# First attention of a two-layer block: value products in fp32 from one exponential, in place of fp32r products of high and low parts

## The reference, cut to what matters

```python
# hidden_states (2, 1024, 512); H = 512, NH = 16 heads, HD = 32
q, k, v = proj(Wq), proj(Wk), proj(Wv)                # (B, NH, S, HD)
q = q * cos + rotate_half(q) * sin
k = k * cos + rotate_half(k) * sin
scores = einsum('bhqd,bhkd->bhqk', q, k) / sqrt(HD)
scores = where(causal, -inf, scores)                  # causal = above the diagonal
attn = softmax(scores, axis=-1)
out = einsum('bhqk,bhkd->bhqd', attn, v)              # the value products
return einsum('bsh,oh->bso', out.reshape(B, S, H), Wo)
```

## Time and profile before

| | us |
|---|---|
| median of 3 runs | 3494.87 |
| lowest, highest | 3492.46, 3495.08 |
| the profiled execution's own time | 3502.3 |
| its span (first to last instruction) | 3500.5 |
| the front, to its last large store | about 0 to 197 |
| loading of the first operands, first row maxima | 197 to 259 |
| the attention's steps, from the first Z product of head 0 to the last value product | 259 to 744 |

### The profile page before, as it was taken

One profiled execution on the slowest core, in us unless ns is written; L12 is line 12 of the kernel. 1 busy time (PEld: TensorE's weight loads), 2 busy tenths in 40 slices (PEclk: granted clock), 3 DMA queues, 4 the chain that ended last, 5 costly groups with the idle time before them and its releaser, 6 DMA issues. The chain is left out here.

```text
span 3500.5 us, 42242 instructions
## 1 busy us (share of the span) xinstructions
PE 2895.0 (83%) x14636; PEld 2302.5 (66%) x14636; DVE 2011.0 (57%) x3642; ACT 1202.6 (34%) x2343; POOL 950.9 (27%) x664
## 2 busy tenths in 40 slices
PE   7938888876999999347899999579999994488994
PEld 6825555554888888236688888467888883366773
DVE  5628778756233232435466666655666666667655
ACT  2206555542111111113344444224444442233331
POOL 1206666653111111203100000140000001267743
PEclk9958889987999999678899999899999997699997
DMA  4542222213000100672000000300000002111002
GB/s 163 196 150 70 81 96 82 76 50 114 19 19 19 36 0 1 189 278 100 26 32 31 21 31 21 131 35 25 32 21 31 21 27 102 67 37 37 0 1 96
DMA packets 111743, 224.36 MB, mean 64 GB/s; under 512 B 9376, under 2 KB 55456, under 8 KB 110848
## 3 DMA queue, kind: packets, MB, share of 16 engines
q1 hardware_dynamic: 111616, 222.72, 18.4%
HBM read 155.84 MB, written 66.58 MB: 64 GB/s over the span
## 5 line engine op out<-in xcount | busy, mean ns | idle before, releaser
L1041 POOL TENSOR_TENSOR l0a_probs_hl<-l0a_probs,l0a_probs_hl 128x896 fp32r<-128x896 f32 (+1 forms) x128 | 293.4, 2311 | 229.6 <-ACT l0a_probs L963 229.6
L1273 PE MATMUL l1a_obank<-l1a_pT_hl,l1k_v_hl 128*128 128x512 f32 (+3 forms) x1152 | 300.4, 370 | 7.2 <-DVE l1a_pT_hl L1346 7.1
L1346 DVE TENSOR_TENSOR l1a_pT_hl<-l1a_work,l1a_pT_hl 128x512 fp32r<-128x512 f32 (+3 forms) x384 | 212.9, 555 | 155.1 <-ACT l1a_pT_hl L1306 154.9
L1299 ACT ACTIVATE l1a_probs<-l1a_scores,l1a_row 128x128 f32<-128x128 f32 (+7 forms) x256 | 189.3, 741 | 317.9 <-DVE l1a_row L1336 317.9
L1253 PE MATMUL l1a_scores<-l1k_kT_hl,l1a_qa_hl 128*128 128x512 f32 (+3 forms) x1152 | 291.6, 361 | 1.5 <-ACT l1a_probs L1299 1.5
L1389 POOL TENSOR_TENSOR l1a_q_stage<-l1k_qpe,l1a_ones 128x512 fp32r<-128x512 f32 x32 | 33.3, 1040 | 875.4 <-PE l1a_work L1281 818.4
L962 ACT ACTIVATE l0a_probs_hl<-l0a_sbank 128x896 fp32r<-128x896 f32 (+1 forms) x192 | 156.2, 813 | 258.9 <-PE l0a_sbank L934 194.8
L1678 DVE TENSOR_TENSOR f0f_hid<-f0f_silu,f0f_ubank 128x512 f32<-128x512 f32 x64 | 44.1, 688 | 322.2 <-PE f0f_ubank L1613 322.2
L1306 ACT CAST l1a_pT_hl<-l1a_work 128x512 fp32r<-128x512 f32 (+3 forms) x384 | 183.6, 478 | 107.3 <-PE l1a_work L1264 106.1
L948 PE MATMUL l0a_obank<-l0a_probs_hl,l0a_v_stage 128*96 128x512 f32 (+3 forms) x768 | 195.6, 380 | 28.3 <-DVE l0a_probs_hl L1002 23.7
L1281 PE MATMUL l1a_work<-l1a_wov,l1a_oT_hl 128*128 128x512 f32 x768 | 214.2, 401 | 5.0 <-DVE l1a_oT_hl L1365 3.0
(11 more groups left out here) (254 smaller groups left out, 6324.6 us busy)
## 6 DMA issues: line engine op xcount, KB each, us to landing
qk_dram<-l0f_stage SPq DMA_DIRECT2D x8, 2048.0 KB, 9.5
l1a_wov<-wov_dram SPq DMA_DIRECT2D x32, 512.0 KB, 3.4
v_dram<-l0f_v_rows SPq DMA_DIRECT2D x16, 768.0 KB, 3.7
l0a_v_stage<-v_dram SPq DMA_DIRECT2D x8, 1536.0 KB, 9.2
l1a_wabs<-wabs_dram SPq DMA_DIRECT2D x32, 384.0 KB, 3.8
l0a_q_stack<-qk_dram SPq DMA_DIRECT2D x32, 256.0 KB
l0a_k_stack<-qk_dram SPq DMA_DIRECT2D x32, 256.0 KB
wov_dram<-w1a_wov SPq DMA_DIRECT2D x16, 512.0 KB, 3.3
```

Source lines behind the costliest of these rows:

```text
L1041: nc.gpsimd.tensor_tensor(probs_hl[:, r, 1, 0:wide], probs[:, r, 0:wide], f32(probs_hl[:, r, 0, 0:wide]), ALU.subtract).then_inc(low_done[ ...
L1273: last = pe.matmul(obank[:, c:SPAN], src["v_hl"][:, a, n, :], pT_hl[:, ring(n, s), b, c:SPAN], start=(n == 0 and i == 0), stop=(n == QT * ...
L1299: nc.scalar.activation(probs[s][:, first:first + wide, :].rearrange("p k c -> p (k c)"), scores[:, n % S_AHEAD, 0:wide * P], ACT.Exp, bias ...
L1346: nc.vector.tensor_tensor(pT_hl[:, r, 1, c:SPAN], work[:, slot, c:SPAN], f32(pT_hl[:, r, 0, c:SPAN]), ALU.subtract).then_inc(work_free[slo ...
```

## The change

The exponential is taken once, in fp32, and PE reads it as it is. The value products become one fp32 matmul for each block of keys in place of two F32R ones, against 33 columns (the 32 values in fp32 and one column of ones) in place of 96. All L parts go, on DVE and on POOL, and the exponential into F32R with them. In part O, DVE copies the 32 output rows straight into place, and ACT copies the one row of sums. The value products run one step later behind the exponential (LAG = 2), and the ring has 5 places. In the front, ACT copies v once and DVE's subtraction goes; v rows are 528 bytes for four heads in place of 1536. In SP's loop, `store_sums` and `load_values` move from k = 3 to k = 4, where they stand behind `load_stack`, and the three group DMAs move one step later.

```diff
-    v_rows = m.sb("v_rows", [P, 2, NH, 3 * HD0], F32R)
+    v_rows = m.sb("v_rows", [P, 2, NH, VW])
...
-                    nc.scalar.copy(v_part(t, 2), in_heads(t)).then_inc(v_high, 1)
+                    nc.scalar.copy(v_rows[:, t % 2, :, 0:HD0], in_heads(t)).then_inc(read[2], 1)
...
-                    else:
-                        dve.wait_ge(v_high, t + 1)
-                        nc.vector.tensor_tensor(v_part(t, 0), in_heads(t), f32(v_part(t, 2)), ALU.subtract
-                                                ).then_inc(read[2], 1)
...
-RING0 = 4
+LAG = 2
+RING0 = LAG + 3
...
-LOWS_BY_DVE = (1, 5)
+VW = HD0 + 1
...
-        if 0 <= i < HEADS * U:
-            yield "L", i, i
-        if 0 <= i - 1 < HEADS * U:
-            yield "P", i, i - 1
-        if 0 <= i - 2 < HEADS * U and (i - 2) % U in (1, U - 1):
-            yield "O", i, 2 * ((i - 2) // U) + ((i - 2) % U == U - 1)
+        p, o = i - LAG, i - LAG - 1
+        if 0 <= p < HEADS * U:
+            yield "P", i, p
+        if 0 <= o < HEADS * U and o % U in (1, U - 1):
+            yield "O", i, 2 * (o // U) + (o % U == U - 1)
...
-                if k == 3 and h >= 1 and (h - 1) % GROUP_HEADS == GROUP_HEADS - 1 and (h - 1) // GROUP_HEADS + 2 < GROUPS:
+                if k == LAG + 2 and h >= 1 and (h - 1) % GROUP_HEADS == GROUP_HEADS - 1 and (h - 1) // GROUP_HEADS + 2 < GROUPS:
                     load_values((h - 1) // GROUP_HEADS + 2)
-                if k == 3 and 0 <= h - 1 < HEADS:
+                if k == LAG + 2 and 0 <= h - 1 < HEADS:
                     store_sums(h - 1)
-                group, late = divmod(i - (U * (GROUP_HEADS - 1) + 9), U * GROUP_HEADS)
+                group, late = divmod(i - (U * (GROUP_HEADS - 1) + 8 + LAG), U * GROUP_HEADS)
...
-                    mine, count = lows_upto(n)
-                    pe.wait_ge(low_done[mine], count)
+                        wait(pe, sums_copied, 2 * (h - 1) + s + 1)
+                    pe.wait_ge(exp_done, n + 1)
                     for kt, c, at, _ in parts:
-                        for part in range(2):
-                            last = pe.matmul(obank[0:3 * HD0, s, c:SPAN],
-                                             v_stage[:, group % 2, kt, j, :],
-                                             probs_hl[:, r, part, at:at + SPAN - c], start=(kt == 0 and part == 0),
-                                             stop=(kt == QT * (s + 1) - 1 and part == 1))
+                        last = pe.matmul(obank[0:VW, s, c:SPAN], v_stage[:, group % 2, kt, j, :],
+                                         probs[:, r, at:at + SPAN - c], start=kt == 0, stop=kt == QT * (s + 1) - 1)
...
-                    nc.scalar.activation(probs_hl[:, r, 0, 0:wide], sbank[:, n % 2, 0:wide], ACT.Exp)
                     nc.scalar.activation(probs[:, r, 0:wide], sbank[:, n % 2, 0:wide], ACT.Exp).then_inc(exp_done, 1)
+                elif kind == "O":
+                    h, s = divmod(n, 2)
+                    act.wait_ge(values_done, h * U + (U if s else 2))
+                    if s == 0 and h >= 2:
+                        act.wait_ge(sums_stored[h % 2], 16 * (h // 2))
+                    nc.scalar.copy(sum_rows[HD0:VW, h % 2, s, :], obank[HD0:VW, s, :]).then_inc(sums_copied, 1)
...
-                    nc.vector.tensor_copy(o_rows[2 * HD0:3 * HD0 + 1, h % 2, s, :], obank[0:HD0 + 1, s, :]
-                                          ).then_inc(o_copied, 1)
-                    dve.wait_ge(o_copied, n + 1)
-                    nc.vector.tensor_tensor(out[j * HD0:(j + 1) * HD0, g, s * SPAN:(s + 1) * SPAN],
-                                            obank[2 * HD0:3 * HD0, s, :], o_rows[2 * HD0:3 * HD0, h % 2, s, :],
-                                            ALU.add).then_inc(o_done, 1)
+                    nc.vector.tensor_copy(out[j * HD0:(j + 1) * HD0, g, s * SPAN:(s + 1) * SPAN], obank[0:HD0, s, :]
+                                          ).then_inc(o_done, 1)
...
-                if kind == "L" and n % U not in LOWS_BY_DVE:
-                    _, _, wide = pieces(n % U)
-                    r = n % RING0
-                    pool.wait_ge(exp_done, n + 1)
-                    nc.gpsimd.tensor_tensor(probs_hl[:, r, 1, 0:wide], probs[:, r, 0:wide],
-                                            f32(probs_hl[:, r, 0, 0:wide]), ALU.subtract).then_inc(low_done[False], 1)
```

More of the change, by code:

```diff
@@ L517, in front_layer0 @@
     stage = m.sb("stage", [P, 2, 2, 2, KT, 2 * P], F32R)
-    v_rows = m.sb("v_rows", [P, 2, NH, 3 * HD0], F32R)
-    ones = m.sb("ones", [P, 1])
+    v_rows = m.sb("v_rows", [P, 2, NH, VW])
     stats, mv = m.sb("stats", [P, NT, 6]), m.sb("mv", [P, NT, 2])
@@ L536, in front_layer0 @@
     use = front_uses()
-    v_part = lambda t, part: v_rows[:, t % 2, :, part * HD0:(part + 1) * HD0]
     in_heads = lambda t: bank[:, t % 2, 2, :].rearrange("p (h d) -> p h d", h=NH)
@@ L673, in _ @@
             nc.vector.memset(eps[:, :], EPS_LN).then_inc(eps_set, 1)
-            nc.vector.memset(ones[:, :], 1.0).then_inc(ones_set, 1)
             for t in range(3):
@@ L677, in _ @@
             normalise(0)
-            dve.wait_ge(ones_set, 1)
             for slot in range(2):
-                nc.vector.tensor_copy(v_rows[:, slot, :, HD0:2 * HD0], ones[:, :, None].to_broadcast([P, NH, HD0])
-                                      ).then_inc(ones_set, 1)
+                nc.vector.memset(v_rows[:, slot, :, HD0:VW], 1.0).then_inc(ones_set, 1)
             for kind, n in front_order():
@@ L724 @@
 U = len(UNITS)
-FIRST, LAST = -2 * U, HEADS * U + 2
+FIRST, LAST = -2 * U, HEADS * U + LAG + 1
 MAX_PARTS = [(t, c) for t in range(TB) for c in range(0, (t + 1) * P, SPAN)]
-LOWS_BY_DVE = (1, 5)
+VW = HD0 + 1
 def pieces(u):
@@ L738, in pieces @@
     return s, out, at
-def lows_upto(unit):
-    h, u = divmod(unit, U)
-    mine = u in LOWS_BY_DVE
-    per = len(LOWS_BY_DVE) if mine else U - len(LOWS_BY_DVE)
-    return mine, h * per + sum((v in LOWS_BY_DVE) == mine for v in range(u + 1))
 def steps_layer0():
@@ L784, in attention_layer0 @@
     probs = m.sb("probs", [P, RING0, 2 * SPAN])
-    probs_hl = m.sb("probs_hl", [P, RING0, 2, 2 * SPAN], F32R)
     negmax = m.sb("negmax", [P, 2, TB])
@@ L789, in attention_layer0 @@
     q_stack, k_stack = (m.sb(n, [P, STACKS, S], F32R) for n in ("q_stack", "k_stack"))
-    v_stage = m.sb("v_stage", [P, 2, TB, GROUP_HEADS, 3 * HD0], F32R)
-    o_rows = m.sb("o_rows", [P, 2, 2, SPAN])
+    v_stage = m.sb("v_stage", [P, 2, TB, GROUP_HEADS, VW])
+    sum_rows = m.sb("sum_rows", [HD0 + 1, 2, 2, SPAN])
     sums = m.sb("sums", [P, 2, GROUP_HEADS * S // P])
@@ L892, in _ @@
                         load_inverse(group)
-            for group in range((HEADS * U + 23 - (U * (GROUP_HEADS - 1) + 9) - 10) // (U * GROUP_HEADS) + 1, GROUPS):
+            for group in range((HEADS * U + 23 - (U * (GROUP_HEADS - 1) + 8 + LAG) - 10) // (U * GROUP_HEADS) + 1, GROUPS):
                 load_sums(group)
@@ L997, in _ @@
                                             f32(negmax_hl[0:TB, n % 2, 0, :]), ALU.subtract).then_inc(m_done, 1)
-                elif kind == "L" and n % U in LOWS_BY_DVE:
-                    _, _, wide = pieces(n % U)
-                    r = n % RING0
-                    dve.wait_ge(exp_done, n + 1)
-                    nc.vector.tensor_tensor(probs_hl[:, r, 1, 0:wide], probs[:, r, 0:wide],
-                                            f32(probs_hl[:, r, 0, 0:wide]), ALU.subtract).then_inc(low_done[True], 1)
                 elif kind == "O":
@@ L1007, in _ @@
                     dve.wait_ge(values_done, h * U + (U if s else 2))
-                    if s == 0 and h >= 2:
-                        dve.wait_ge(sums_stored[h % 2], 16 * (h // 2))
-                    nc.vector.tensor_copy(o_rows[2 * HD0:3 * HD0 + 1, h % 2, s, :], obank[0:HD0 + 1, s, :]
-                                          ).then_inc(o_copied, 1)
-                    dve.wait_ge(o_copied, n + 1)
-                    nc.vector.tensor_tensor(out[j * HD0:(j + 1) * HD0, g, s * SPAN:(s + 1) * SPAN],
-                                            obank[2 * HD0:3 * HD0, s, :], o_rows[2 * HD0:3 * HD0, h % 2, s, :],
-                                            ALU.add).then_inc(o_done, 1)
-                group, late = divmod(i - (U * (GROUP_HEADS - 1) + 9), U * GROUP_HEADS)
+                    nc.vector.tensor_copy(out[j * HD0:(j + 1) * HD0, g, s * SPAN:(s + 1) * SPAN], obank[0:HD0, s, :]
+                                          ).then_inc(o_done, 1)
+                group, late = divmod(i - (U * (GROUP_HEADS - 1) + 8 + LAG), U * GROUP_HEADS)
                 if kind == "P" and late == 6 and 0 <= group < GROUPS - 1:
```

17 lines of the change are left out of this document (8 added, 9 removed).

## The result

The changed kernel takes 3535.38 us, median of 4 runs (3529.51 to 3536.44), beside 3494.97 us for the kernel before on the same chip: a ratio of 1.0112, 95% interval 1.0094 to 1.0129. It is slower by 1.1%. The prediction was 3498 us, range 3462 to 3522. The profiled execution took 3529.51 us (span 3527.7, clock 0.929); its rows follow.

A forecast was written before the change was run, and what follows sets the result against it. PE, at 14.2 us a head, was taken to bound the attention. On the profiled 3502.3 us, -28.1 there, +37 from SP's queue, -4.5 and -1.2 gave 3505.5; less 7.4 for the median, 3498, range 3462 to 3522.

The forecast's parts named there:

- PE needs 14.2 us a head: PE in attention: 6.4 us for N, Z and M plus 7.8 for fp32 value products, at full clock.
- the term that was put at nothing: PE's value products: 33 weight columns in place of 96 save nothing visible, since loads run beside the stream.
- The slot of an fp32 record: PE's value products: one fp32 record of 512 columns takes 0.43 us from start to start.
- The fuller-PE rival: Value and score products on PE: fresh weights or unhidden transitions make a head 15.0 us, 3524 in all; chance 0.18.
- The stall: SP's queue: sums' store behind operands and values delays the next head's maxima's rows in six heads; 37 us.
- Waits on DVE: PE's waits in attention for maxima, their join and low parts: all put at nothing after the change.
- The clock: Attention stretch: with PE's queue full, the granted clock was expected at 1.00 outside of real gaps.
- The start: Wait for the first maxima's rows 4.5 us shorter, and the front 1.2 us shorter.
- The sum: Whole kernel: -28.1 + 37 - 4.5 - 1.2 = +3.2 us on the profiled 3502.3, so 3505.5.
- waits in every head: Z products on PE: operands needing 15.5 us delay maxima's rows in 26 heads, 3511 to 3538; chance 0.12.
- the small stall: SP's queue: the sums' store misses the operands or lands within 9 us, 3461 to 3476 in all; chance 0.32.
- the sixth Z product's 7.4 us: PE's timeline: the sixth Z product, behind which the operands are issued, is done 7.4 us after a head's N.

The follow-up runs named there:

- the fastest version: Changed kernel with 96 weight columns, sums stored ahead of operands, loads of sums and later values behind the next head's maxima's rows: 3466.74 us, 0.9923 of the kernel before.

## Why the prediction was wrong

- **The step that failed** is "PE needs 14.2 us a head", and in it the term that was put at nothing: 33 columns of weights in place of 96, "since loads run beside the stream". That they save nothing is right. But at the ends of the value products the loads don't run beside the stream with 33 columns, and that costs 1.6 us a head (15.87 against 14.26 us). With 96 columns the 14.2 us hold. The slot of an fp32 record was right: 0.429 us at 512 columns, 0.43 predicted. The fuller-PE rival had the mechanism in a few words ("transitions that I have taken as hidden"), with 15.0 us and 3524; the trace of before could not show it, as its value products were F32R.
- **The stall** was right in place and cause: load of sums 9.5 us behind N against 9.7, Z product 12.4 against 12.6, six heads, lower clock behind it. Its price was 37 us and came out at 22, since PE at 15.9 us a head wants the rows later. At the pace that I had assumed it costs 41 (96 columns).
- **Waits on DVE** fell to 1.0 us, as forecast at nothing.
- **The clock** was forecast at 1.00 outside of gaps. It is 1.00 in the ordinary head above and 0.97 over the stretch, with the gaps in it.
- **The start** came 8.1 us earlier against 5.7.
- **The sum**: 30.25 heads by 1.67 us is +50, the stall -15, the start -2.4: 33 us on the forecast of 3505.5 for a profiled execution give 3538, which took 3529.5; behind the last value product, where the change does nothing, this execution took 2747.7 us against 2758.2 before, which no term foresaw; without these 10.5 us the sum is 1 to 2 us short. The median came out 37 us over the forecast of 3498. The other rivals: waits in every head did not come (six in all); the small stall did not either. (In the working of the stall, the sixth Z product's 7.4 us are 7.3 by their own terms; nothing hangs on it.)

## What to carry to other kernels

Where fp32 products with up to 64 columns of weights alternate with products of other kinds, count the ways in and out as well as the products, and try 65 or more columns by reading on into neighbouring data. (65 gave the shortest heads here, 14.09 us, but it was run once and not with the new order of the queue.) When an engine is relieved, follow the queue that issues the next head's transfers: here the sums' store was worth 21 us alone and 19 us at the faster pace, and there moving two loads as well was worth 15 more. Take an experiment's verdict from the stretch that it should move, not from its total.

## What the runs showed of the hardware

- fp32 products with 33 or 64 columns of weights start 0.16 us behind a bf16 product of 128 columns, with 65 to 128 columns 0.07, and F32R ones with 33 columns 0.04. Behind them the next product starts 0.42 us after a last record of 384 columns, whose slot inside is 0.32; with 96 columns it starts 0.03 us behind. With 33 and 64 columns the weight loads at these places begin with their products; with 65 to 128 the first one begins with the mask product. What in TensorE does this the records don't show; the number of columns is also that of the result's rows, and the two were not tried apart.
- An issue that takes SP 0.2 to 0.7 us otherwise took 7.9 to 9.3 us as the sixth DMA behind four of operands and one of values, whichever it was: in five groups of six the sums' store with the order of the changed kernel, in all six their load with the store moved ahead. In the sixth group of the changed kernel the store's issue took 1.49 us (at 667.76), and the load of sums still came only at 681.95, with a head of 20.3 us: there the stall comes from the store's landing and not from the long issue. In the fastest version, which issues the values behind the load of sums, and in the kernel before, whose values stand ahead of the operands, no issue of the stretch takes longer than 0.9 us. What makes the issue long wasn't tested.
- 768 KB of operands kept about two of the 16 DMA engines busy (share 0.13 from 340 to 344 us), with packets of 4096 bytes that took 0.16 us each, and a one-row store of 4 KB issued behind them and the values started 13.3 us after its issue.
